# A Perceiver block on one core: group results copied by ScalarE, divisions moved behind all row maxima, six logits banks near the end, and three quarters of the output projection in f16

## The reference

```python
x = x + _L0_xattn_ref(_layernorm(x), ctx_1024, mask, ...)   # stage 0
x = x + _L0_attn_ref(_layernorm(x), ...)                    # stage 1
x = x + _L0_ffn_ref(_layernorm(x), ...)                     # stage 2
# stage 3, _L1_xattn_ref(q=_layernorm(x), kv=ctx_1024, Wq, Wkv, Wc): 16 heads of 32
qp = einsum('bld,ed->ble', q, Wq)
idx = argmax(einsum('bld,bmd->blm', qp, kv), axis=-1)       # over 8192 context rows
mem = take_along_axis(kv, idx[..., None], axis=1)           # 512 gathered rows
mk, mv = split(einsum('bld,ed->ble', mem, Wkv), 2, axis=-1) # one key and value head of 32
attn = softmax(einsum('bhld,bmd->bhlm', qh, mk) / sqrt(32)) # 16 heads x 512 x 512
out = einsum('bhlm,bmd->bhld', attn, mv)                    # -> [512, 512]
x = x + einsum('bld,ed->ble', out, Wc)
x = x + _L1_attn_ref(_layernorm(x), ...)                    # stage 4
x = x + _L1_ffn_ref(_layernorm(x), ...)                     # stage 5
```

## Time and profile before

| | us |
|---|---|
| median of 3 runs (1124.36, 1124.47, 1129.54) | 1124.47 |
| the profiled execution: its own time | 1123.12 |
| its span in the trace | 1121.4 |
| PE / DVE / ACT / POOL busy, share of the span | 93% / 73% / 44% / 37% |
| chain that ended last: PE / DVE / ACT / POOL | 72% / 18% / 4% / 2% |

### The profile page before, as it was taken

How to read it: one execution, slowest core, us unless ns; L and a number is a source line. 1 busy time by engine, 2 the same in 40 slices (tenths; PEclk the granted TensorE clock), 3 DMA queues, 4 the chain that set the end, 5 groups by cost and what they waited for, 6 DMA issues and landing times.

```text
span 1121.4 us, 14657 instructions
## 1 busy us (share of the span) xinstructions
PE 1037.9 (93%) x4905; PEld 486.1 (43%) x4905; DVE 820.3 (73%) x1180; ACT 489.5 (44%) x731; POOL 414.9 (37%) x229
## 2 busy tenths in 40 slices
PE   7999999999999989999569999999998799888997
PEld 3444444444444444544224344444542144466453
DVE  5566676799999467585974399999677557476896
ACT  2345555666666637336771210010034615256164
POOL 4287777300000544000010376676228920084003
PEclk9999999999999999999879999999999999999999
DMA  6145554632443256320020254456100010000001
GB/s 235 72 140 196 171 163 159 225 113 88 174 150 112 101 198 227 113 93 2 1 76 0 97 230 171 163 200 190 37 1 1 17 62 1 1 1 1 2 1 38
DMA packets 41831, 112.65 MB, mean 100 GB/s; under 512 B 4512, under 2 KB 15296, under 8 KB 35648
## 3 DMA queue, kind: packets, MB, share of 16 engines
q1 hardware_dynamic: 38592, 101.13, 25.6%
q10 hardware_dynamic: 2880, 9.96, 2.7%
q0 software_dynamic: 320, 1.05, 0.3%
HBM read 103.18 MB, written 7.34 MB: 99 GB/s over the span
## 4 chain that ended last, share of the span: by engine, by line
PE 72%; DVE 18%; ACT 4%; issue 3%; POOL 2%; DMA 1%; DVEq 0%; SPq 0%; POOLq 0%; ACTq 0%
PE PS L767 5%; PE PS L768 5%; PE PS L769 5%; PE PS L798 5%; PE PS L800 5%; PE PS L799 5%; PE PS L1677 4%; PE PS L1678 4%; PE PS L1679 4%; PE PS L249 4%; PE PS L251 4%; PE PS L250 4%; DVE arena L2034 2%; DVE arena L1604 2%; PE PS L739 1%
## 5 line engine op out<-in xcount | busy, mean ns | idle before, releaser
L798 PE MATMUL PS<-arena 128*128 128x512 f16 x256 | 97.0, 379 | 2.4 <-DVE arena L689 1.3
L767 PE MATMUL PS<-arena 128*128 128x512 f16 x256 | 97.0, 379 | 2.0 <-DVE arena L616 2.0
L1677 PE MATMUL PS<-arena 128*128 128x512 f16 x256 | 97.0, 379 | 1.8 <-DVE arena L1527 1.8
L769 PE MATMUL PS<-arena 128*128 128x512 f16 x256 | 97.0, 379 | 0.0
L1678 PE MATMUL PS<-arena 128*128 128x512 f16 x256 | 97.0, 379 | 0.0
L768 PE MATMUL PS<-arena 128*128 128x512 f16 x256 | 97.0, 379 | 0.0
L1679 PE MATMUL PS<-arena 128*128 128x512 f16 x256 | 97.0, 379 | 0.0
L799 PE MATMUL PS<-arena 128*128 128x512 f16 x256 | 97.0, 379 | 0.0
L800 PE MATMUL PS<-arena 128*128 128x512 f16 x256 | 97.0, 379 | 0.0
L623 DVE TENSOR_TENSOR arena<-PS,arena 128x512 f32<-128x512 f32 x64 | 43.6, 681 | 58.1 <-ACT arena L547 58.1
L243 PE MATMUL PS<-IDENTB 128*128 128x512 bf16 x245 | 62.9, 401 | 21.9 <-DVE SM L1253 21.9
(11 more groups left out here) (370 smaller groups left out, 2446.2 us busy)
## 6 DMA issues: line engine op xcount, KB each, us to landing
arena<-in_ctxT SPq DMA_DIRECT2D x32, 1024.0 KB, 6.2
arena<-in_ctx SPq DMA_DIRECT2D x16, 1024.0 KB, 5.4
arena<-in_w ACTq DMA_DIRECT2D x8, 1024.0 KB, 5.7
arena<-in_w SPq DMA_DIRECT2D x8, 1024.0 KB, 6.8
XN<-in_ffnGU SPq DMA_DIRECT2D x16, 384.0 KB, 3.4
XN<-in_WinT SPq DMA_DIRECT2D x16, 290.0 KB, 5.0
gu_hi<-arena SPq DMA_DIRECT2D x16, 192.0 KB, 3.5
gu_lo<-arena SPq DMA_DIRECT2D x16, 192.0 KB, 3.6
```

Of the source, the lines that this page charges most:

```text
L767: pe.matmul(bank, CHI[:, b, e, cols], QHI[:, e, :], start=(e == 0), stop=False)
L769: ins = pe.matmul(bank, CLO[:, b, e, cols], QHI[:, e, :], start=False, stop=(e == DT - 1))
L798: pe.matmul(PS[:, t, :], PHI[:, j, cols], CHI[:, b, j, :], start=False, stop=False)
L1677: pe.matmul(bank, QHI3[:, e, cols], CHI3[:, b, e, :], start=(e == 0), stop=False)
```

## The change

- DVE's two copies out of banks 7 and 6 go to ACT (`take_group`), behind the exponential of unit 22, 38 and 54.
- `weighted(g)` for the first three groups moves behind DVE's last entry, and makes f16 high and low parts of `ATTT` too. `DEN` gets one slice a group.
- `STEPS` places the entries earlier, the shift entry behind unit 7 of a group and not 9; ACT's `shift_hi` comes behind unit 8 and not 10. The shift entry uses transposes in place of f32 matmuls.
- From unit 46 on the logits use six banks (4, 5, 0, 1, 2, 3).
- `WC1` is scaled by 64 and split into f16 high and low parts (ACT, GpSimd) before the units; `add_tile` scales back.
- The projection of the first three quarters (c = 0 to 2) is done in f16, three products each, before the last quarter, which stays f32. The last group's reciprocal and product are cut into four slices of 128 columns. The 18 filling matmuls go.
- GpSimd's 44 adds stay as they are.

```diff
-        STEPS = (0, 2, 4, 6, 9, 10, 12, 14, 15)
+        STEPS = (0, 2, 3, 5, 7, 9, 11, 13, 14)
+        WIDE = 44
+        RING = (4, 5, 0, 1, 2, 3)
+        def logits_bank(n):
+            return 4 + n % 2 if n < WIDE else RING[(n - WIDE) % len(RING)]
...
+            pool.wait_ge(act_marks, ACT_MARK["s3_wc_hi"])
+            pool.wait_ge(s3_kv_psum, 2)
+            pool.tensor_tensor(WC_LO, WC1, WC_HI, ALU.subtract).then_inc(pool_marks, 1)
             for n in range(UNITS):
...
+            def take_group(g):
+                act.wait_ge(pe_marks, PE_MARK[f"s3_sums{g}"])
+                act.copy(DEN[:, g, :], PS[:, 7, :]).then_inc(s3_den, 1)
+                act.wait_ge(s3_pv, 4 * g + 4)
+                act.copy(ATTT[:, g, :], PS[:, 6, :]).then_inc(s3_den, 1)
+            act.activation(WC1, WC1, ACT.Copy, scale=W_UP).then_inc(act_marks, 1)
+            act.wait_ge(act_marks, ACT_MARK["s3_wc_up"])
+            act.copy(WC_HI, WC1).then_inc(act_marks, 1)
             shift_hi(0)
...
-                act.activation(PT[:, n % 16, :], PS[:, 4 + n % 2, :], ACT.Exp).then_inc(s3_p, 1)
-                if n % 16 == 10 and n // 16 < GROUPS - 1:
+                act.activation(PT[:, n % 16, :], PS[:, logits_bank(n), :], ACT.Exp).then_inc(s3_p, 1)
+                if n % 16 == 6 and n > 16:
+                    take_group(n // 16 - 1)
+                if n % 16 == 8 and n // 16 < GROUPS - 1:
                     shift_hi(n // 16 + 1)
...
             def weighted(g):
+                dve.wait_ge(s3_den, 2 * g + 2)
+                dve.reciprocal(DEN[:, g, :], DEN[:, g, :]).then_inc(s3_attt, 1)
+                dve.tensor_tensor(ATTT[:, g, :], ATTT[:, g, :], DEN[:, g, :], ALU.mult)
+                dve.tensor_copy(ATTT_HI[:, g, :], ATTT[:, g, :])
+                dve.tensor_tensor(ATTT_LO[:, g, :], ATTT[:, g, :], ATTT_HI[:, g, :], ALU.subtract)
+            def weighted_last(g):
...
+                for t in range(NT):
+                    cols = slice(t * P, (t + 1) * P)
+                    dve.reciprocal(DEN[:, g, cols], PS[:, 7, cols])
+                    dve.tensor_tensor(ATTT[:, g, cols], PS[:, 6, cols], DEN[:, g, cols], ALU.mult)
...
-                if n % 16 == 6 and n > 16:
-                    weighted(n // 16 - 1)
-            weighted(GROUPS - 1)
+            for g in range(GROUPS - 1):
+                weighted(g)
+            weighted_last(GROUPS - 1)
...
-                if n >= 2:
+                if n == WIDE + 2:
+                    for r in range(2):
+                        pe.wait_ge(s3_taken[r], ENTRIES // 2)
+                elif n >= WIDE + 6:
+                    pe.wait_ge(s3_p, n - 5)
+                elif 2 <= n < WIDE + 2:
                     pe.wait_ge(s3_p, n - 1)
...
-            fill(pe, 5, 18)
-            pe.wait_ge(s3_attt, DT)
-            for t in range(NT):
-                for c in range(DT):
-                    ins = pe.matmul(PS[:, 4 + t, :], ATTT[:, c, t * P:(t + 1) * P], WC1[:, c, :], ...)
+            def out_early(t):
+                for c in range(DT - 1):
+                    pe.matmul(PS[:, 4 + t, :], ATTT_HI[:, c, rows], WC_HI[:, c, :], start=(c == 0), stop=False)
+                    pe.matmul(PS[:, 4 + t, :], ATTT_HI[:, c, rows], WC_LO[:, c, :], start=False, stop=False)
+                    pe.matmul(PS[:, 4 + t, :], ATTT_LO[:, c, rows], WC_HI[:, c, :], start=False, stop=False)
+            def out_last(t):
+                pe.wait_ge(s3_attt, 4 * (GROUPS - 1) + 2 * t + 2)
+                pe.matmul(PS[:, 4 + t, :], ATTT[:, DT - 1, ...], WC1[:, DT - 1, :], start=False, stop=True)
+            out_early(0)
+            out_early(1)
+            out_last(0)
+            out_last(1)
...
+            for t in range(2, NT):
+                out_early(t)
+                out_last(t)
+                turn_tile(pe, 4, t - 2)
```

More of the change, by code:

```diff
@@ L173, in perceiver_kernel @@
                           "s5_out_scale")
[L174 to L175 removed]
+        ACT_MARK = marks("s1_std", "s3_mks_hi", "s3_wc_up", "s3_wc_hi", "s4_softplus", "s4_ela", "s4_std_early", "s4_std_last")
+        POOL_MARK = marks("s0_primed", "const_ready", "s1_wall", "s3_primed", "s3_iota", "s3_ones", "s3_wc", "s4_pad", "s4_select", "s4_wout")
         pe_marks = sem("pe_marks")
@@ L1330, in perceiver_kernel @@
         MEMIDX = view(174 * K + 64, [NT], U32)
-        NMAX = view(174 * K + 512, [DT, NT, 4])
+        NMAX = view(177 * K, [DT, NT, 4])
         MEM = view(154 * K, [NT, D])
@@ L1338, in perceiver_kernel @@
         ATTT = view(138 * K, [DT, N])
-        DEN = view(154 * K, [N])
+        DEN = view(154 * K, [DT, N])
+        ATTT_HI = view(162 * K, [DT - 1, N], F16)
+        ATTT_LO = view(166 * K, [DT - 1, N], F16)
+        WC_HI = view(172 * K, [DT, D], F16)
+        WC_LO = view(94 * K, [DT, D], F16)
         ACC = [view(86 * K, [4, N]), XT]
@@ L1615, in weighted @@
             def weighted(g):
+                dve.wait_ge(s3_den, 2 * g + 2)
+                dve.reciprocal(DEN[:, g, :], DEN[:, g, :]).then_inc(s3_attt, 1)
+                dve.wait_ge(s3_attt, 4 * g + 1)
+                dve.tensor_tensor(ATTT[:, g, :], ATTT[:, g, :], DEN[:, g, :], ALU.mult).then_inc(s3_attt, 1)
+                dve.wait_ge(s3_attt, 4 * g + 2)
+                dve.tensor_copy(ATTT_HI[:, g, :], ATTT[:, g, :]).then_inc(s3_attt, 1)
+                dve.wait_ge(s3_attt, 4 * g + 3)
+                dve.tensor_tensor(ATTT_LO[:, g, :], ATTT[:, g, :], ATTT_HI[:, g, :], ALU.subtract).then_inc(s3_attt, 1)
+            def weighted_last(g):
                 dve.wait_ge(s3_pv, 4 * g + 4)
                 dve.wait_ge(pe_marks, PE_MARK[f"s3_sums{g}"])
[L1619 to L1630, removed]
+                for t in range(NT):
+                    cols = slice(t * P, (t + 1) * P)
+                    dve.reciprocal(DEN[:, g, cols], PS[:, 7, cols]).then_inc(s3_attt, 1)
+                    dve.wait_ge(s3_attt, 4 * g + 2 * t + 1)
+                    dve.tensor_tensor(ATTT[:, g, cols], PS[:, 6, cols], DEN[:, g, cols], ALU.mult).then_inc(s3_attt, 1)
             def take_entry(e):
@@ L1740, in entry @@
                     for t in range(NT):
-                        ins = pe.matmul(PS[0:4, bank, t * P:(t + 1) * P], NMAX[:, g, t, :], IDENT[:, :],
-                                        start=True, stop=True)
+                        ins = pe.transpose(PS[0:4, bank, t * P:(t + 1) * P], NMAX[:, g, t, :], IDENT[:, :])
                 ins.then_inc(s3_entry, 1)
@@ L1761, in weigh @@
                 if m == 0 and g:
-                    pe.wait_ge(s3_den, 3 * (g - 1) + 2)
+                    pe.wait_ge(s3_den, 2 * (g - 1) + 2)
                 for j in range(4):
@@ L1772, in sums @@
                 if g:
-                    pe.wait_ge(s3_den, 3 * (g - 1) + 1)
+                    pe.wait_ge(s3_den, 2 * (g - 1) + 1)
                 for j in range(4):
@@ L1777, in sums @@
                 if last:
+                    pe.wait_ge(s3_p, UNITS)
                     for j in range(4):
@@ L1799, in s3_pe @@
             sums(GROUPS - 1)
-            fill(pe, 5, 18)
-            pe.wait_ge(s3_attt, DT)
-            for t in range(NT):
-                for c in range(DT):
[L1804 to L1808, removed]
+            pe.wait_ge(pool_marks, POOL_MARK["s3_wc"])
+            pe.wait_ge(s3_attt, 4 * (GROUPS - 1))
+            def out_early(t):
+                rows = slice(t * P, (t + 1) * P)
+                for c in range(DT - 1):
[4 more added lines that the diff above has]
+                pe.wait_ge(s3_attt, 4 * (GROUPS - 1) + 2 * t + 2)
+                pe.matmul(PS[:, 4 + t, :], ATTT[:, DT - 1, t * P:(t + 1) * P], WC1[:, DT - 1, :],
+                          start=False, stop=True).then_inc(out_psum, 1)
+            out_early(0)
+            out_early(1)
+            out_last(0)
+            out_last(1)
+            pe.wait_ge(s3_attt, 4 * (GROUPS - 1) + 2 * NT)
+            for t in range(2, NT):
+                out_early(t)
+                out_last(t)
+                turn_tile(pe, 4, t - 2)
+            turn_tile(pe, 4, NT - 2)
             fill(pe, 4, 10)
```

4 lines of the change are left out of this document (2 added, 2 removed).

## The result

| us | before | after |
|---|---|---|
| median of 5 runs each (lowest to highest) | 1124.36 (1122.17 to 1129.54) | 1116.90 (1115.73 to 1118.99) |
| profiled execution: its own time / its span | 1123.12 / 1121.4 | 1115.73 / 1114.0 |
| first add, last add's end | 834.24, 896.51 | 833.84, 896.54 |
| last row sums known to DVE, last normalised tile | 898.65, 920.61 | 898.66, 914.27 |

The account below looks back on a forecast made before the run. GpSimd's adds up to 896.5 us and the serial tail behind them were taken as the bound. Tail -5.6, adds -0.4, clock falls +2.1 and +1.1 gave -2.8: 1121.7 us, range 1117.0 to 1126.5.

Parts of the forecast that it names:

- tail: Serial work from DVE's last reciprocal to the last normalised tile: 21.96 us falls to 16.35, gain 5.6.
- adds' run: GpSimd's 44 adds from 834.24 us: end at 896.1 instead of 896.51, contention included and clock left out, gain 0.4.
- contention: DVE's SBUF instructions slow GpSimd's adds, 0.46 us per two-input meeting, 1.2 a group; 2.4 charged, bounds 0 and 4.1.
- fall at `sums(2)`: PE idles 6 us before the third row sums, its clock drops to 1.2 GHz: loss 2.1 us.
- fall at `sums(0)`: PE waits 2.6 us before the first row sums, its clock may drop: up to 2.4, half taken, loss 1.1.
- Rival 1: The clock costs nothing or nearly: -6.0 us, 1118.5, down to 1116.5 with less contention; chance 0.30.
- Rival 3: DVE's division queue is late, groups of 8.65 us, so the tail starts 0.6 later: 1122.3 us; chance 0.08.
- Rival 4: PE's clock is at the lower level at all four row sums, price 9.3: +3.3 us, 1127.8; chance 0.12.
- Rival 2: The SBUF port shared by DVE and GpSimd locks for whole instructions: 1.1 us worse, 1122.8; chance 0.08.

Follow-up runs that it names:

- no_port: fill_all with the division and f16 parts of groups 0 to 2 on 8 of 512 columns, output not the reference's: 1114.91 us, ratio 0.9916.
- fill_all: The changed kernel with 9, 5, 23 and 7 filling matmuls on PE ahead of the four row sums: 1115.99 us, ratio 0.9929.
- fill_sums2: The changed kernel with 23 filling matmuls on PE ahead of the third row sums only: 1116.08 us, ratio 0.9912.
- after_again: The changed kernel itself, unchanged, run on a second chip: 1118.44 us, ratio 0.9952.
- order_only: The changed kernel with the old tail (no f16 parts, one 512-column reciprocal, 18 fillings, f32 projection): 1124.40 us, ratio 0.9994.
- two_banks: The changed kernel with logits in two banks throughout, no six banks from unit 46 on: 1118.03 us, ratio 0.9938.
- pe_m3: The changed kernel with PE summing every group's last key tile, so GpSimd makes 32 adds, not 44: 1109.53 us, ratio 0.9884.

## Why the prediction was wrong

The two terms, the adds and the tail, were the right ones, and so were the things that act on them; wrong was how much the adds were charged. Each number here is of the profiled executions.

| step | predicted | measured |
|---|---|---|
| tail | 16.35 us, gain 5.6 | 15.61 us, gain 6.35 |
| first add | 834.2 | 833.84, gain 0.4 (0.3 of it from ahead of the attention) |
| adds' run, clock and contention left out | 896.1 - 2.4 - 834.24 = 59.5 | 59.54 (no_port), 58.8 by estimate without the fillings' delay |
| contention | 2.4 | at least 1.1 (fill_all less no_port), 1.8 by estimate |
| the two rows above together | 61.9 | 60.63 (fill_all, fill_sums2) |
| fall at `sums(2)` | 2.1 | 2.07 (after less fill_sums2), some 1.3 in after_again |
| fall at `sums(0)` | 1.1 (half of up to 2.4) | 0 here, 1.5 to 1.6 where it came |
| stages 4 and 5 | 0 | gain 1.1 here |

**The step that failed is the clock and contention charge on the adds**, and there the two terms "at `sums(0)` ... I take half: loss 1.1" and "Contention ... 1.2" a group. From -2.8 the parts lead to the measured -7.4: -1.1 for `sums(0)`, -1.2 for contention and the adds' own run, -0.75 for the tail, -0.4 for the start, -1.1 for the later stages. The last two, 1.5 us, are for the most part no work of the change, but differences between executions.

- *`sums(0)`.* The wait was as forecast in kind (2.32 for 2.6), but half of a price is a value that no execution shows: it is 0, or 1.5 to 1.6. It came in after_again, order_only and two_banks and not in after or fill_sums2. It does not explain why the second chip gained 5.6 and the first pair 7.5: the two profiled executions of the changed kernel differ by 2.6 in span, of which 0.3 lies before the first add, 0.84 in the adds and 1.5 behind the last tile. What made the medians differ stays open.
- *Contention.* The loss per two-input meeting, 0.46, holds (1.72 for 1.27); a cast's is about 0.2, not 0.25. I counted nine meetings, 3.6, took one group's 1.2 as covered and charged 2.4. The traces of fill_all and no_port have 2.5 for all nine, since the second cast (884.29) falls into a wait of GpSimd and the last subtraction (894.47) has no add behind it. Some 0.7 of the 2.5 falls into waits of group 3 (in order_only 0.46 of 0.83). With contention the adds' run was forecast at 61.9 and measured at 60.63; of the 1.2 between them contention has 0.6 by the estimate above, and the adds themselves, which come every 1.23 and not 1.25, the rest. With no_port's 59.54 as it stands, contention has all of it. (In the sum for group 1, 848.9 + 15 + 1.67 is 865.6, not 865.65, which changes nothing.)
- *The tail.* A slice takes 4.76 / 4 = 1.19 us, not 1.3, and a tile 2.65, not 2.78. I had summed lengths and put 0.03 between them; in the trace an instruction can start a little before the end of the one ahead (the second reciprocal is 0.94 to 0.96 long and has 0.87 on the chain). Spacings, not lengths, are to be summed.
- *Rival 1* had the size (-6.0) by the wrong reason: the clock did cost 2.07 at `sums(2)`. *Rival 3* failed: the third group's last instruction ended at 897.1, 2.6 later than forecast but before the row sums were known at 898.6, though the three groups took 6.3 to 7.9 us, not 6.5. *Rival 4* is not seen in after; two_banks' profiled execution comes nearest.
- *Rival 2* was judged too quickly. The lock is there. A cast of 8 columns takes 0.17 alone and 1.20 beside the adds, and 1.20 + 0.03 is the spacing of the adds, 14.75 / 12 = 1.23: each such cast, product or subtraction waits until the running add is over. The Trainium skill (SBUF — State Buffer, "SBUF: two separate sides") says just that of a GpSimd instruction and a VectorE one with two SBUF inputs or in a 2-port mode: whichever starts first has the shared pair for its whole instruction and the other fully blocks. The trace agrees for VectorE's wait. For GpSimd's it is less: an instruction of 0.69 that runs beside it costs it 0.46, one of 8 columns nothing. An instruction of 8 columns takes 0.17, so the other columns of the 0.69 take 0.52, and the 0.46 is near that; whether only the first and last part of an instruction is free of the lock, no run separates. The rule's price of 1.1 on top of the 2.4 was not there: the whole loss was 1.1 to 1.8.
- *Later stages.* I gave them 0. With nothing changed in them, from the last normalised tile to the end the traces have 199.7 (after), 200.8 (before), 201.6 (fill_sums2), 201.9 (fill_all), 201.2 (after_again), 199.7 (order_only) and 198.1 (pe_m3). So one pair of profiled executions can't show a difference of 1 or 2 us at its end. The run of adds is steadier where the clock does not fall in it (60.63 in both fill_sums2 and fill_all); where it falls, it moves too (62.70 and 63.54 for one program).

## What to carry to other kernels

Judge a change on one engine's queue by what it puts ahead of the instruction that others wait for: the same tail gained nothing behind two extra instructions ahead of `shift_lo`, 3.1 us with them moved, and 5.6 to 7.5 with the whole order changed (3.1 and 5.6 have intervals that overlap). Charge contention only where the engine that loses has no wait behind it. Fillings keep the clock, but count them: where the wait got shorter, in no_port, 23 of them held the row sums by 0.70. And when an engine's run of adds sets the end, take adds away: moving twelve of them to PE (pe_m3) gained more than all the rest (8.9 us on top of 5.6), and took away PE's waits for GpSimd but the last; in its one trace the clock did not fall in the attention.

## What the runs showed of the hardware

- TensorE's clock behind a wait of 2.3 us: in two executions of one program, with waits of 2.32 and 2.34 at the same place, it stayed at 1.00 in one and went to 0.52 in the other. Behind 5.27 it fell in both, and behind 5.08 (order_only) and 3.70 (two_banks) too. How soon it came back differed: `weigh` behind `sums(2)` took 1.94 in one and 1.40 in the other, and in two_banks the granted clock was still 0.50 over 896 to 900. Filling matmuls in the wait kept it at 1.00 and gave back 2.07 us.
- VectorE's casts, products and subtractions from SBUF to SBUF beside GpSimd's adds wait for the add to end, whatever their width: 1.20 us for 8 columns, 1.38 for a cast of 512, and 0.17 for 8 columns between two adds. Only what is ready just as an add ends is quick, as the changed kernel's product at 875.24 (0.69). A product from PSUM of 128 columns ran at 0.29.
- The reciprocal is the costliest of VectorE's simple operations here, 0.95 for 128 columns and 3.35 for 512, and from SBUF to SBUF it did not get longer beside GpSimd's adds (3.33 to 3.35 for 512 columns, 0.13 to 0.20 for 8).
